# A soft mixture of experts: the first layer of experts 1 to 7 from seven block products instead of eight

## The chip, the cores and the metric

The kernel runs on one core of a Trainium2 chip. The metric is device microseconds of one execution, launch to end. The kernel before takes 835.61 us, the median of 3 runs (835.45 to 835.63).

## The reference, cut to what matters

Eight sequences of 512 tokens and width 256 go through an attention layer and then a soft mixture of 8 experts. Its first half makes dispatch and combine weights and gives each expert 128 slots per sequence, 1024 slots in all. Then, for every expert e:

```
h  = einsum('besd,edh->besh', slots, w1) + b1      # 1024 slots, 256 -> 1024
h  = gelu(h)
eo = einsum('besh,ehd->besd', h, w2) + b2          # 1024 -> 256
out = einsum('bmd,bnm->bnd', eo, combine)
```

The last layer norm takes each row's mean away, so the kernel centres w2 and b2 over the output width beforehand (subtracts each row's mean). Arithmetic is float32. TensorE is given each operand as two float32r parts, a rounded high part and the low part that the rounding left, and three passes are summed: high x high, high x low, low x high (`PASSES`).

## The kernel before, in words

The engines' programs are written out one after the other by hand; there is no scheduler. Each engine runs its instructions in the written order and waits on semaphores. The stages are attention (to about 160 us), dispatch and combine weights (to 380 us), the experts (380 to 737 us) and the combine stage (to the end). The change touches the experts.

An expert has two halves f of 512 slots (four sequences each). `KH` is 8, the number of 128-wide blocks of the hidden width, `KD` is 2, the number of 128-deep blocks of the input width. For each of its 16 tiles i = (f, j) TensorE makes a hidden tile of 128 hidden units x 512 slots (`hidden`, L1014): 2 input blocks x 3 passes = 6 matmuls of 512 columns. ScalarE applies gelu from PSUM into `act` (L1495) and rounds it into the high part of `act_r` (L1500). VectorE subtracts to get the low part (`rest_of_act`, L2121). Two tiles later TensorE multiplies it with w2 (`expert_out`): for each of 4 sequences one matmul of 512 columns, the activation's high part against both parts of w2 side by side (L1044), and one of 256 columns, its low part against w2's high part (L1047). Only the first half of expert 0 uses three matmuls of 256 columns instead (`narrow_out`, L1022). After the last block VectorE adds the two column halves and the bias into `slots_eo` (`keep_eo`, L2144 and L2150, 8 instructions a half).

Beside that, for the expert after, VectorE sums w2's rows (L2173) and subtracts their mean (L2184), ScalarE rounds both weights (L1465) and VectorE makes their low parts (L2078); VectorE also rounds and splits the slots (L2085, L2089). Rounded weights have two sets of tiles, one for each parity of the expert; the loops hold two experts. GpSimd does nothing in this stage: its last work is in the stage before, where it scales dispatch weights (L617), makes low parts of y (L624) and centres rows (L630). SP (the DMA queue's engine) loads the raw weights of an expert when those of the one before are split.

## Time and profile before

| what | us |
|---|---|
| median of 3 runs | 835.61 |
| the profiled execution, its own time | 835.44 |
| its span, first to last instruction | 833.3 |
| TensorE busy | 826.1 (99%) |
| VectorE busy | 643.3 (77%) |
| ScalarE busy | 548.2 (66%) |
| GpSimd busy | 86.7 (10%) |

Shares of busy time are averages over the four stages. The granted TensorE clock is 1.00 of full speed (2.4 GHz) in every stretch. A matmul's shown duration is longer than its pace, since the next starts before it ends; the pace is read from the chain of waits.

### The profile page before, as it was taken

Reading aid. Unit: us, or ns where it says so; the run is one execution under the profiler, and the core shown is the slowest. Engines: PE = TensorE matmul, PEld = TensorE weight load, DVE = VectorE, ACT = ScalarE, POOL = GpSimd, SP = SyncE. Lnnn points to the kernel's source line nnn. Section 1 sums busy time; section 2 is a strip of 40 time slices with the busy share of each in tenths; the row PEclk is TensorE's granted clock in tenths of the full one; section 3 lists DMA queues with packets and bytes.
Section 4 is the critical chain, followed back from the end, with each engine's and each line's share of the span. In section 5 each row is a group of like instructions: output and inputs, shape, how many; then the busy total and the mean of one; then the engine's idle time right before and its main releaser. Section 6 shows DMA issues by size and latency. Waiting matters only on the chain.

```text
span 833.3 us, 14932 instructions
## 1 busy us (share of the span) xinstructions
PE 826.1 (99%) x4866; PEld 717.7 (86%) x4866; DVE 643.3 (77%) x1293; ACT 548.2 (66%) x1078; POOL 86.7 (10%) x103
## 2 busy tenths in 40 slices
PE   8999999999999999999999999999999999999997
PEld 8989999888888888878888888888888888899997
DVE  8788888899999999998867666665766665477776
ACT  5676766657787887689555565555555554568775
POOL 0300000033223334350000000000000000000000
PEclk9999999999999999999999999999999999999999
DMA  6111131102223252225030202020110203066893
GB/s 209 59 51 52 53 99 33 45 28 101 102 94 121 98 192 102 76 77 203 1 102 0 101 1 101 0 98 3 45 55 2 99 1 101 1 217 210 282 292 111
DMA packets 52562, 75.38 MB, mean 90 GB/s; under 512 B 3104, under 2 KB 33696, under 8 KB 52384
## 3 DMA queue, kind: packets, MB, share of 16 engines
q1 hardware_dynamic: 52512, 74.76, 26.8%
q8 instruction: 26, 0.43, 0.2%
q14 instruction: 24, 0.20, 0.1%
HBM read 49.59 MB, written 25.17 MB: 90 GB/s over the span
## 4 chain that ended last, share of the span: by engine, by line
PE 96%; DVE 2%; ACT 1%; issue 1%; DMA 0%; ACTq 0%; DVEq 0%
PE bank L1014 21%; PE bank L1044 13%; PE bank L1086 11%; PE bank L883 10%; PE bank L908 10%; PE bank L1047 7%; PE bank L892 3%; PE bank L750 3%; PE bank L800 3%; PE bank L693 2%; PE bank L773 2%; PE bank L761 2%; PE bank L783 2%; PE bank L715 1%; PE bank L726 1%; PE bank L1022 1%
## 5 line engine op out<-in xcount | busy, mean ns | idle before, releaser
L1014 PE MATMUL bank<-snT,w_r 128*128 128x512 f32 x768 | 194.7, 393 | 0.0
L1495 ACT ACTIVATE act<-bank,b_sb 128x512 f32<-128x512 f32 x128 | 88.0, 687 | 139.3 <-PE bank L1014 138.9
L2121 DVE TENSOR_TENSOR act_r<-act,act_r 128x512 fp32r<-128x512 f32 x128 | 88.3, 691 | 110.7 <-ACT act_r L1500 110.6
L1044 PE MATMUL bank<-w_r,act_r 128*128 128x512 f32 x480 | 173.1, 396 | 0.0
L1014 PEld LDWEIGHTS bank<-snT,w_r 128*128 128x128 f32 x768 | 136.5, 188 | 28.8 <-issue 0.3
L1047 PE MATMUL bank<-w_r,act_r 128*128 128x256 f32 x480 | 134.6, 280 | 0.0
L1044 PEld LDWEIGHTS bank<-w_r,act_r 128*128 128x128 f32 x480 | 90.2, 188 | 21.0
L908 PE MATMUL bank<-disp_r,y_r 128*128 128x512 f32 x384 | 103.4, 406 | 0.4 <-DVE disp_r L1974 0.3
L883 PE MATMUL bank<-yT_r,snT 128*128 128x512 f32 x384 | 99.4, 395 | 0.0
L1047 PEld LDWEIGHTS bank<-w_r,act_r 128*128 128x128 f32 x480 | 90.6, 189 | 4.1
L1086 PE MATMUL bank<-eo_r,comb_r 128*128 128x258 f32 x768 | 92.3, 282 | 0.0
L1086 PEld LDWEIGHTS bank<-eo_r,comb_r 128*128 128x128 f32 x768 | 92.2, 189 | 0.1
L1500 ACT ACTIVATE act_r<-act 128x512 fp32r<-128x512 f32 x128 | 80.9, 632 | 12.0
L883 PEld LDWEIGHTS bank<-yT_r,snT 128*128 128x128 f32 x384 | 71.7, 188 | 15.9 <-issue 0.5
L908 PEld LDWEIGHTS bank<-disp_r,y_r 128*128 128x128 f32 x384 | 67.7, 189 | 12.8 <-DVE disp_r L1974 0.8
L1367 ACT ACTIVATE disp<-neg_lt,neg_max 128x512 f32<-128x512 f32 x56 | 40.5, 723 | 35.6 <-DVE neg_lt L1940 35.4
L617 POOL TENSOR_SCALAR disp<-disp,rz_disp 128x512 f32<-128x512 f32 x56 | 39.6, 707 | 123.9 <-DVE rz_disp L1969 123.9
L1974 DVE TENSOR_TENSOR disp_r<-bank,disp_r 128x512 fp32r<-128x512 f32 x64 | 43.6, 682 | 5.0 <-ACT disp_r L1379 4.4
L1394 ACT ACTIVATE comb<-comb,zero_col 128x512 f32<-128x512 f32 x64 | 45.3, 715 | 1.6 <-DVE comb L1963 1.4
L1379 ACT ACTIVATE disp_r<-bank 128x512 fp32r<-128x512 f32 x64 | 37.4, 585 | 10.7 <-PE bank L892 10.7
L1940 DVE TENSOR_SCALAR_CACHE_REDUCE neg_lt<-bank 128x512 f32<-128x512 f32 x56 | 38.3, 684 | 4.7 <-DVE comb L1963 2.5
L2078 DVE TENSOR_TENSOR w_r<-stage,w_r 128x1024 fp32r<-128x1024 f32 x32 | 38.9, 1218 | 0.0
(203 smaller groups left out, 1311.3 us busy)
## 6 DMA issues: line engine op xcount, KB each, us to landing
combine_scratch<-comb SPq DMA_DIRECT2D x64, 256.0 KB, 2.0
stage<-in_w SPq DMA_DIRECT2D x16, 1024.0 KB, 6.3
stage<-combine_scratch SPq DMA_DIRECT2D x4, 2048.0 KB, 9.0
snT<-combine_scratch SPq DMA_DIRECT2D x4, 2048.0 KB, 9.6
x_scratch<-stage SPq DMA_DIRECT2D x8, 512.0 KB, 3.2
x<-x_scratch SPq DMA_DIRECT2D x8, 512.0 KB, 3.9
x_d<-x_scratch SPq DMA_DIRECT2D x8, 512.0 KB, 9.5
slots_eo<-in_x SPq DMA_DIRECT2D x7, 512.0 KB, 4.4
```

The source lines that it names most:

```text
L883: last = pe.matmul(bank[m % 2][:, :], snT[:, i, k, m * S:(m + 1) * S], yT_r[:, j, k, :], start=(n == 0), stop=(n == len(steps) - 1))
L908: last = pe.matmul(bank[4 + k][:, :], y_r[:, i, t, k * P:(k + 1) * P], disp_r[h][:, j, t, :], start=(n == 0), stop=(n == len(fill_steps) - 1))
L1014: last = pe.matmul(hidden_bank(e, i)[:, :], w1_r[q][:, a, k, j * P:(j + 1) * P], sl_r[f][:, c, k, :], start=(n == 0), stop=(n == len(steps ...
L1044: pe.matmul(bank[BH + c][:, :].rearrange("p (w d) -> p w d", w=2), act_r[:, i % RING, 0, c * S:(c + 1) * S], w2_r[q][:, :, j, :], start=(j ...
L1047: pe.matmul(bank[BH + c][:, 0:D], act_r[:, i % RING, 1, c * S:(c + 1) * S], w2_r[q][:, 0, j, :], start=False, stop=(j == KH - 1), skip_gro ...
L1086: done = pe.matmul(bank[4 * u + t][:, 0:DZ], comb_r[:, m % RING, i, t * P:(t + 1) * P], eo_r[u][:, j, m, :], start=(m == 0 and n == 0), st ...
L1367: act_fn(dispatch(b, m), neg_logits(b, m), ACT.Exp, bias=least, scale=-1.0, accum_out=total).then_inc(disp_exp, 1)
L1394: act_fn(comb[:, m % RING, :], comb[:, m % RING, :], ACT.Exp, bias=zero_col[:], scale=-1.0)\
L1495: act_fn(act[:, i % 2, :], hidden_bank(e, i)[:, :], ACT.Gelu, bias=b1_sb[:, ds(e * KH + i % KH, 1)])\
L1500: act_fn(act_r[:, i % RING, 0, :], act[:, i % 2, :], ACT.Copy).then_inc(h_hi, 1)
L1974: v.tensor_tensor(disp_r[h][:, 1, :, cols], bank[2 + m % 2][:, :].rearrange("p (t s) -> p t s", t=NT), disp_r[h][:, 0, :, cols].bitcast(F3 ...
L2121: v.tensor_tensor(act_r[:, i % RING, 1, :], act[:, i % 2, :], act_r[:, i % RING, 0, :].bitcast(F32), ALU.subtract).then_inc(h_split, 1)
```

## The change

Expert 0 stays as it was, but for its second half, whose second layer now also uses three matmuls of 256 columns. In experts 1 to 7 the first layer is cut into a 2 x 2 x 2 block problem: two input blocks k, two halves f of the slots, and hidden blocks in pairs (g, g + 4), so that a `group` g of 4 has four hidden tiles. Winograd's form of Strassen's scheme makes these four tiles from seven products instead of eight. A product (`product`) is 3 matmuls of 512 columns over one 128-deep block.

- The operands of the products are sums: three sums of slots and S1 to S4 of w1's blocks. GpSimd makes them: 4 subtractions of 128x512 for an expert (`combine_slots`) and 4 of 128x128 for each group (`combine_w1`).
- ScalarE rounds them (w1: 128x512 and 128x384 a group; slots: two pairs and two singles an expert), VectorE makes the low parts. The slots' last operand is rounded by VectorE (`split_last_operand`).
- Four products run into one chain bank (bank 0 or 2 by the group's parity). On the way ScalarE copies the partial sum three times (`keep_part`): into bank 3, into the tile `act[3]` or `act[4]`, into `act[2]`. VectorE adds bank 1 to the two copies in SBUF (`add_tile`). Gelu then reads bank 3, `act[2]`, the chain bank and `act[3]` or `act[4]`.
- w2 is centred while it is rounded: ScalarE's Identity takes minus the mean as bias, VectorE's low part adds it in one scalar_tensor_tensor. The instruction L2184 goes.
- `expert_out` is three matmuls of 256 columns for each sequence and tile, 12 a tile, and the four banks 4 to 7 hold both halves, so `keep_eo` is 2 instructions of 128x512 a half. The rounded w2 has one set of tiles instead of two. The loops hold one expert, in groups of four.

On TensorE a group reads: P0, P3, out tile 0 of the group before, P1, P2, out tile 1, P4, out tile 2, P5, P6, out tile 3. P1 and P2 wait for the first copy, P4 for the second, P5 for the third, P6 for `add_tile` 0, and P3 of the next group for `add_tile` 1 (both use bank 1).

```diff
+        ORDER = [0, 3, 1, 2, 4, 5, 6]
+        TILE_OF = [0, 2, 1, 3]
+        OUT_NEEDS = [1, 3, 3, 4]
+        ALL_PRODUCTS = HALVES * KH + (E - 1) * GROUPS * PRODUCTS
...
+            def combine_slots(e):
+                if not is_batch(e, 1):
+                    pool.wait_ge(sl_split, right_through(e - 1, 5))
+                t1, t2, t3, t4 = sl_sum[:, 3], sl_sum[:, 0], sl_sum[:, 1], sl_sum[:, 2]
+                at = 4 * (e - 1)
...
+                nc.gpsimd.tensor_tensor(t3, slots_raw(e, 1, 1), slots_raw(e, 0, 1), ALU.subtract)\
+                    .then_inc(sl_summed, 1)
+                pool.wait_ge(sl_summed, at + 1)
+                alone(pool)
+                nc.gpsimd.tensor_tensor(t1, slots_raw(e, 0, 1), slots_raw(e, 0, 0), ALU.subtract)\
+                    .then_inc(sl_summed, 1)
+                pool.wait_ge(sl_summed, at + 2)
+                alone(pool)
+                nc.gpsimd.tensor_tensor(t2, slots_raw(e, 1, 1), t1, ALU.subtract).then_inc(sl_summed, 1)
+                pool.wait_ge(sl_summed, at + 3)
+                alone(pool)
+                nc.gpsimd.tensor_tensor(t4, slots_raw(e, 1, 0), t2, ALU.subtract).then_inc(sl_summed, 1)
...
+            def combine_w1(e, g):
+                pool.wait_ge(w_loaded[0], 16 * (e + 1))
+                if not is_batch(e, 1) or g >= 2:
+                    pool.wait_ge(w_split[0], fills_through(e, g - 2, 2))
+                s2, s3, s4 = [w1_sum[:, g % 2, n, :] for n in range(3)]
...
+            def expert(e, last=False):
+                combine_w1(e, 1)
+                combine_w1(e, 2)
+                if not last:
+                    combine_slots(e + 1)
+                combine_w1(e, 3)
+                if not last:
+                    combine_w1(e + 1, 0)
...
+            def product(e, g, n):
+                if n in (0, 2):
+                    pe.wait_ge(w_split[0], fills_through(e, g, 1 + n // 2))
+                if g == 0:
+                    pe.wait_ge(sl_split, right_through(e, 1 if is_batch(e, 1) and n == 0 else [2, 2, 3, 2, 4, 4, 5][n]))
+                if n == 3 and is_batch(e, 1) and g == 0:
+                    pe.wait_ge(h_act, HALVES * KH - 1)
+                elif n == 3:
+                    pe.wait_ge(tile_added, added_through(e, g, 0))
+                elif n in (1, 2, 4, 5):
+                    pe.wait_ge(part_kept, parts_through(e, g, {1: 1, 2: 1, 4: 2, 5: 3}[n]))
+                elif n == 6:
+                    pe.wait_ge(tile_added, added_through(e, g, 1))
+                x = chain_bank(g)
+                target = [x, bank[3], x, bank[1], x, x, bank[1]][n]
+                for s, (a, c) in enumerate(PASSES):
+                    done = pe.matmul(target[:, :], w1_op[:, g % 2, a, LEFT_AT[n], :], slot_operand(n)[:, c, :],
+                                     start=(n in (0, 3) and s == 0), stop=(s == 2), skip_group_check=True)
+                done.then_inc(h_in_psum, 1)
...
+            def expert_out(e, g, a):
+                pe.wait_ge(h_split, tiles_through(e, g, OUT_NEEDS[a]))
+                if a == 0:
+                    pe.wait_ge(w_split[1], w2_through(e, g + 1))
+                if g == 0 and a % 2 == 0:
+                    pe.wait_ge(eo_ready, e * HALVES * BH - (BH if a == 0 else 0))
+                j = g + GROUPS if a in (1, 2) else g
+                out_rows(a // 2, a, j, g == 0 and a % 2 == 0, g == GROUPS - 1 and a % 2 == 1)
+            def expert_group(e, g, before):
+                product(e, g, 0)
+                product(e, g, 3)
+                before(0)
+                product(e, g, 1)
+                product(e, g, 2)
+                before(1)
+                product(e, g, 4)
+                before(2)
+                product(e, g, 5)
+                product(e, g, 6)
+                before(3)
...
+            def keep_part(e, g, i):
+                sc.wait_ge(h_in_psum, products_through(e, g, [1, 4, 5][i]))
+                if i == 1:
+                    sc.wait_ge(h_split, tiles_through(e, g, -1))
+                to = [bank[3][:, :], kept_tile(g, 3), act[:, 2, :]][i]
+                act_fn(to, chain_bank(g)[:, :], ACT.Copy).then_inc(part_kept, 1)
+            def gelu(e, g, i):
+                tile = TILE_OF[i]
+                source = [bank[3][:, :], act[:, 2, :], chain_bank(g)[:, :], kept_tile(g, 3)][i]
+                if i in (0, 2):
+                    sc.wait_ge(h_in_psum, products_through(e, g, 3 if i == 0 else 6))
+                    sc.wait_ge(h_split, tiles_through(e, g, 0 if i else -1 if is_batch(e, 1) and g == 0 else -3))
+                else:
+                    sc.wait_ge(tile_added, added_through(e, g, 1 + i // 2))
+                j = g + GROUPS if i in (1, 2) else g
                 alone(sc)
-                act_fn(act[:, i % 2, :], hidden_bank(e, i)[:, :], ACT.Gelu, bias=b1_sb[:, ds(e * KH + i % KH, 1)])\
-                    .then_inc(h_act, 1)
-                sc.wait_ge(h_act, n + 1)
-                if i >= RING or not first:
-                    sc.wait_ge(eo_steps, (n - RING + 1) * BH)
-                act_fn(act_r[:, i % RING, 0, :], act[:, i % 2, :], ACT.Copy).then_inc(h_hi, 1)
+                act_fn(kept_tile(g, tile), source, ACT.Gelu, bias=b1_sb[:, ds(e * KH + j, 1)]).then_inc(h_act, 1)
...
+            def rest_of_w1(e, g, step):
+                dve.wait_ge(w_hi[0], fills_through(e, g, step + 1))
+                cols = slice(4 * step, 4 + 3 * step)
+                v.tensor_tensor(w1_op[:, g % 2, 1, cols, :], w1_sum[:, g % 2] if step else w1_direct(g),
+                                w1_op[:, g % 2, 0, cols, :].bitcast(F32), ALU.subtract).then_inc(w_split[0], 1)
...
+            def expert_group(e, g, first=False, last=False):
+                keep_part(e, g, 0)
+                if g == 0:
+                    cast_pair(e, 1)
+                if g:
+                    gelu(e, g - 1, 3)
+                    round_tile(e, g - 1, 3)
+                elif not first:
+                    gelu(e - 1, GROUPS - 1, 3)
+                    round_tile(e - 1, GROUPS - 1, 3)
+                if 0 < g < GROUPS - 1:
+                    round_w1(e, g + 1, 0)
+                    round_w1(e, g + 1, 1)
+                elif g and not last:
+                    cast_slots(e + 1, 3)
+                    cast_pair(e + 1, 0)
+                keep_part(e, g, 1)
+                gelu(e, g, 0)
+                round_tile(e, g, 0)
+                keep_part(e, g, 2)
+                if g == 0:
+                    round_w1(e, 1, 0)
+                    round_w1(e, 1, 1)
+                if g < 2:
+                    round_w2(e, g)
+                elif g == GROUPS - 1 and not last:
+                    round_w1(e + 1, 0, 0)
+                    round_w1(e + 1, 0, 1)
+                gelu(e, g, 1)
+                round_tile(e, g, 1)
+                if g == 1:
+                    round_w2(e, 2)
+                gelu(e, g, 2)
+                round_tile(e, g, 2)
+                if g == 1:
+                    round_w2(e, 3)
+                if g == GROUPS - 1 and not last:
+                    cast_slots(e + 1, 2)
...
+            def add_tile(e, g, i):
+                tile = 2 + i
+                dve.wait_ge(part_kept, parts_through(e, g, 3))
+                if i:
+                    dve.wait_ge(h_in_psum, products_through(e, g, 7))
+                v.tensor_tensor(kept_tile(g, tile), bank[1][:, :], kept_tile(g, tile), ALU.add).then_inc(tile_added, 1)
...
+                if g:
+                    rest_of_tile(e, g - 1, 3)
+                elif not first:
+                    rest_of_tile(e - 1, GROUPS - 1, 3)
+                if g == 0:
+                    split_last_operand(e)
+                elif g < GROUPS - 1:
+                    rest_of_w1(e, g + 1, 0)
+                    rest_of_w1(e, g + 1, 1)
+                elif not last:
+                    rest_of_operand(e + 1, 3)
+                    rest_of_pair(e + 1, 0)
+                rest_of_tile(e, g, 0)
+                add_tile(e, g, 0)
+                if g == 0:
+                    if not first:
+                        keep_eo(e - 1, 0)
+                    rest_of_w1(e, 1, 0)
+                    rest_of_w1(e, 1, 1)
+                elif g == 1:
+                    rest_of_w2(e, 1)
+                elif g == GROUPS - 1 and not last:
+                    rest_of_w1(e + 1, 0, 0)
+                add_tile(e, g, 1)
+                if g == 0:
+                    rest_of_w2(e, 0)
+                rest_of_tile(e, g, 1)
+                if g == 1:
+                    rest_of_w2(e, 2)
+                    rest_of_w2(e, 3)
+                elif g == 2 and not last:
+                    sum_rows(e + 1, 0)
+                elif g == GROUPS - 1 and not last:
+                    rest_of_w1(e + 1, 0, 1)
+                    rest_of_operand(e + 1, 2)
```

The first place where instructions move is TensorE's program at the head of an expert in the loop, before (`w1_r1`: rounded w1 of the odd expert; bank 4 to 7: outputs):

```order
L1014 MATMUL bank0<-snT,w1_r1 128x512 [waits h_act]
L1014 MATMUL bank0<-snT,w1_r1 128x512 x5
L1030 ISA
L1044 MATMUL bank4<-w2_r0,act_r 128x512 [waits h_split]
L1047 MATMUL bank4<-w2_r0,act_r 128x256
L1044 MATMUL bank5<-w2_r0,act_r 128x512
L1047 MATMUL bank5<-w2_r0,act_r 128x256
```

and now, from P5 of group 0 to the first output tile in group 1 (`w1_op`: operands from w1; `w1_first`: slot operands 4 to 6):

```order
L1201 MATMUL bank0<-w1_first,w1_op 128x512 [waits part_kept]
L1201 MATMUL bank0<-w1_first,w1_op 128x512 x2
...
L1201 MATMUL bank1<-w1_first,w1_op 128x512 [waits tile_added]
L1201 MATMUL bank1<-w1_first,w1_op 128x512 x2
...
L1201 MATMUL bank2<-snT,w1_op 128x512 [waits w1_split]
...
L1201 MATMUL bank1<-snT,w1_op 128x512 [waits tile_added]
...
L1211 ISA [waits w2_split]
L1159 MATMUL bank4<-w2_r,act_r 128x256 [waits eo_ready]
```

Where a hidden tile waited only for gelu and an output tile only for its activation, the products now wait for copies (`part_kept`), additions (`tile_added`) and, at a group's head, for the split weights.

The second place is VectorE's program around the end of group 0, before (one tile's low part after another, with the weights of the next expert between them):

```order
L2121 TENSOR_TENSOR act_r<-act,act_r 128x512 [waits h_hi]
L2182 REGISTER_ALU
L2184 TENSOR_TENSOR stage<-stage,w_mean 128x1024 [waits w2_summed]
L2120 REGISTER_ALU
L2121 TENSOR_TENSOR act_r<-act,act_r 128x512 [waits h_hi]
L2077 REGISTER_ALU
L2078 TENSOR_TENSOR w_r<-stage,w_r 128x1024 [waits w1_hi]
```

and now, from the low part of tile 0 of group 0 to that of tile 2 (L2454), with both `add_tile` (L2448), `keep_eo` (L2466), the low parts of w1's next group (L2406) and of w2 (L2413):

```order
L2454 TENSOR_TENSOR act_r<-act,act_r 128x512 [waits h_hi]
...
L2448 TENSOR_TENSOR act<-bank,act 128x512 [waits part_kept]
...
L2466 TENSOR_TENSOR slots_eo<-bank,b_bc 128x512
...
L2466 TENSOR_TENSOR slots_eo<-bank,b_bc 128x512
...
L2406 TENSOR_TENSOR w_op<-stage,w_op 128x512 [waits w1_hi]
L2404 REGISTER_ALU
L2406 TENSOR_TENSOR w_op<-w_sum,w_op 128x384 [waits w1_hi]
L2447 ISA [waits part_kept]
L2448 TENSOR_TENSOR act<-bank,act 128x512 [waits h_in_psum]
L2411 REGISTER_ALU
L2413 SCALAR_TENSOR_TENSOR w_r<-stage,w_mean,w_r 128x256 [waits w2_hi]
```

The second `add_tile` stands behind two instructions on w1 and the first rows of w2 behind it. The third place is GpSimd, whose program had nothing here and now holds, for the slots of the next expert, behind the last split of this expert's slots (`sl_split`):

```order
L736 ISA [waits sl_split]
L736 ISA
L736 TENSOR_TENSOR sl_sum<-slots_eo 128x512
...
L740 TENSOR_TENSOR sl_sum<-slots_eo 128x512
L742 REGISTER_ALU
L744 TENSOR_TENSOR sl_sum<-slots_eo,sl_sum 128x512 [waits sl_summed]
...
L747 TENSOR_TENSOR sl_sum<-slots_eo,sl_sum 128x512
```

Each waits for the one before it. Behind them stand the w1 sums of group 3.

## Rows read from the trace of the kernel before

**Rows 1.** The page, part 1: busy us, share of the span, instructions.

```profile
PE 826.1 (99%) x4866; PEld 717.7 (86%) x4866; DVE 643.3 (77%) x1293; ACT 548.2 (66%) x1078; POOL 86.7 (10%) x103
```

**Rows 2.** Stages: busy us of PE, PEld, DVE, ACT, POOL; clock; DMA share; GB/s.

```profile
450.00:500.00 50.00, 50.00 (x253) 42.19 (x253) 33.69 (x55) 28.48 (x42) 0.00 (x0) 1.00 0.13 43
```

**Rows 3.** Chain that ended last, in order of time: start, us, what.

```profile
392.76 2.87 PE bank L1022 x24
...
405.53 2.75 PE bank L1014 x12
...
433.37 1.40 PE bank L1014 x6
...
455.65 1.40 PE bank L1014 x6
```

**Rows 4.** Groups by line and form, 420 to 730 us: busy, mean ns, idle before.

```profile
L2121 DVE TENSOR_TENSOR act_r<-act,act_r 128x512 fp32r<-128x512 f32 x112 | 77.4, 691 | 101.6 <-ACT act_r L1500 101.5
L1495 ACT ACTIVATE act<-bank,b_sb 128x512 f32<-128x512 f32 x111 | 76.3, 688 | 128.0 <-PE bank L1014 128.0
L1500 ACT ACTIVATE act_r<-act 128x512 fp32r<-128x512 f32 x111 | 70.1, 632 | 11.4
L2078 DVE TENSOR_TENSOR w_r<-stage,w_r 128x1024 fp32r<-128x1024 f32 x25 | 30.5, 1218 | 0.0
L1465 ACT ACTIVATE w_r<-stage 128x1024 fp32r<-128x1024 f32 x24 | 25.1, 1046 | 0.0
```

**Rows 5.** Groups by line and form, whole span: other prices.

```profile
L1379 ACT ACTIVATE disp_r<-bank 128x512 fp32r<-128x512 f32 x64 | 37.4, 585 | 10.7 <-PE bank L892 10.7
...
L1963 DVE TENSOR_TENSOR comb<-neg_lt,bank 128x512 f32<-128x512 f32 x56 | 37.4, 674 | 0.2
...
L1818 DVE SCALAR_TENSOR_TENSOR stage<-stage,rstd,slots_eo 128x256 f32<-128x256 f32 x32 | 13.9, 489 | 1.4 <-DVE rstd L1814 0.9
...
L1403 ACT ACTIVATE w_row<-stage 128x256 f32<-128x256 f32 x8 | 3.3, 408 | 0.0
...
L2129 DVE TENSOR_TENSOR slots_eo<-bank,b_bc 128x512 f32<-128x512 f32 x2 | 1.3, 684 | 0.0
```

**Rows 6.** Timeline at 502 us, loop of experts: start, us, engine, instruction.

```profile
502.54 0.63 ACT L1500 ACTIVATE act_r<-act 128x512 fp32r<-128x512 f32 x1
...
503.08 1.05 ACT L1465 ACTIVATE w_r<-stage 128x1024 fp32r<-128x1024 f32 x1
503.20 0.69 DVE L2121 TENSOR_TENSOR act_r<-act,act_r 128x512 fp32r<-128x512 f32 x1 [0.74 <-ACT act_r L1500]
503.81 1.22 DVE L2078 TENSOR_TENSOR w_r<-stage,w_r 128x1024 fp32r<-128x1024 f32 x1
...
504.22 0.39 PE L1044 MATMUL bank<-w_r,act_r 128*128 128x512 f32 x1
...
504.51 0.69 ACT L1495 ACTIVATE act<-bank,b_sb 128x512 f32<-128x512 f32 x1 [0.39 <-PE bank L1014]
...
505.32 0.63 ACT L1500 ACTIVATE act_r<-act 128x512 fp32r<-128x512 f32 x1
```

**Rows 7.** Timeline of GpSimd, 192 to 253 us.

```profile
194.55 1.30 POOL L624 TENSOR_TENSOR y_r<-y,y_r 128x512 fp32r<-128x512 f32 x1
...
250.66 1.72 POOL L624 TENSOR_TENSOR y_r<-y,y_r 128x512 fp32r<-128x512 f32 x1
252.69 0.69 POOL L617 TENSOR_SCALAR disp<-disp,rz_disp 128x512 f32<-128x512 f32 x1 [0.30 <-DVE rz_disp L1969]
```

**Rows 8.** Timeline of VectorE, 194 to 254 us.

```profile
194.82 1.58 DVE L1954 TENSOR_TENSOR run_min<-run_min,neg_lt 128x512 f32<-128x512 f32 x1
...
250.34 0.89 DVE L1954 TENSOR_TENSOR run_min<-run_min,neg_lt 128x512 f32<-128x512 f32 x1
251.16 0.68 DVE L1974 TENSOR_TENSOR disp_r<-bank,disp_r 128x512 fp32r<-128x512 f32 x1
...
253.58 0.68 DVE L1954 TENSOR_TENSOR run_min<-run_min,neg_lt 128x512 f32<-128x512 f32 x1
```

More of the change, by code:

```diff
@@ L1050, in expert @@
-            def expert(e, q, first=False):
-                for i in range(HALVES * KH):
-                    if i % KH != 3:
-                        hidden(e, q, i, first)
-                    if i % KH == 2 and not (first and i == 2):
-                        hidden(e, q, i + 1, first)
-                    if first and i == 3:
-                        hidden(e, q, i, first)
-                    for n in FIRST_OUTS.get(i, [i - 2]) if first else [i - 2]:
-                        if n >= 0:
-                            expert_out(e, q, n, first)
-                        else:
-                            expert_out(e - 1, 1 - q, HALVES * KH + n)
@@ L1065, in _ @@
-            expert(0, 0, first=True)
-            with pe.Fori(0, E // 2 - 1) as it:
-                expert(2 * it + 1, 1)
-                expert(2 * it + 2, 0)
-            expert(E - 1, 1)
-            for i in range(2):
-                expert_out(E - 1, 1, HALVES * KH - 2 + i)
+                out_rows(f, i % RING, j, j == 0, j == KH - 1)
+            for i in range(HALVES * KH):
+                if i % KH != 3:
+                    hidden(i)
+                if i % KH == 2 and i != 2:
+                    hidden(i + 1)
+                if i == 3:
+                    hidden(i)
+                for n in FIRST_OUTS.get(i, [i - 2]):
+                    first_out(n)
@@ new lines, in expert @@
+            def expert(e, first=False):
+                if first:
+                    product(e, 0, 0)
+                    first_out(HALVES * KH - 2)
+                    product(e, 0, 3)
+                    product(e, 0, 1)
+                    product(e, 0, 2)
+                    first_out(HALVES * KH - 1)
+                    product(e, 0, 4)
+                    product(e, 0, 5)
+                    product(e, 0, 6)
+                else:
+                    expert_group(e, 0, lambda a: expert_out(e - 1, GROUPS - 1, a))
+                for g in range(1, GROUPS):
+                    expert_group(e, g, lambda a: expert_out(e, g - 1, a))
@@ L1074, in combine @@
+            expert(1, first=True)
+            with pe.Fori(2, E) as e:
+                expert(e)
+            for a in range(TILES):
+                expert_out(E - 1, GROUPS - 1, a)
             def combine(b, u, last=False):
@@ L1538, in _ @@
-            expert(0, 0, first=True)
-            with sc.Fori(0, E // 2 - 1) as it:
-                expert(2 * it + 1, 1)
-                expert(2 * it + 2, 0)
-            expert(E - 1, 1, last=True)
-            experts_finished(sc)
+            for i in range(HALVES * KH):
+                activate(i)
+                if i == 0:
+                    keep_slots(B - 1, 1, 1)
+                if i == KH:
+                    weights_finished(sc)
+                    round_w1(1, 0, 0)
+                    round_w1(1, 0, 1)
+                if i == KH + 3:
+                    cast_pair(1, 0)
@@ new lines, in _ @@
+            for g in range(GROUPS):
+                expert_group(1, g, first=(g == 0))
+            with sc.Fori(2, E - 1) as e:
+                for g in range(GROUPS):
+                    expert_group(e, g)
+            for g in range(GROUPS):
+                expert_group(E - 1, g, last=True)
+            gelu(E - 1, GROUPS - 1, 3)
+            round_tile(E - 1, GROUPS - 1, 3)
+            sc.wait_ge(h_in_psum, ALL_PRODUCTS)
+            sc.wait_ge(w_split[1], w2_through(E, 0))
+            round_eo(0, 0, 0)
@@ L1545, in square_mix @@
+            for m in range(BEGUN_COMBINE):
+                round_combine(0, 0, m, True)
+            sc.wait_ge(eo_ready, E * HALVES * BH - BH)
+            round_eo(0, 0, 1)
             def square_mix(b, u, t):
@@ L1557, in combine @@
             def combine(b, u, first=False, last=False):
-                for m in range(BEGUN if first else 0, E):
+                for m in range(BEGUN_COMBINE if first else 0, E):
                     round_combine(b, u, m, first)
@@ new lines, in _ @@
+            for g in range(GROUPS):
+                expert_group(1, g, first=(g == 0))
+            with dve.Fori(2, E - 1) as e:
+                for g in range(GROUPS):
+                    expert_group(e, g)
+            for g in range(GROUPS):
+                expert_group(E - 1, g, last=True)
+            rest_of_tile(E - 1, GROUPS - 1, 2)
+            rest_of_tile(E - 1, GROUPS - 1, 3)
+            dve.wait_ge(h_in_psum, ALL_PRODUCTS)
+            pad_eo(0)
+            rest_of_eo(dve, 0, 0, 0)
@@ L2270, in combine @@
             def combine(b, u, first=False, last=False):
-                for m in range(BEGUN if first else 0, E):
+                for m in range(BEGUN_COMBINE if first else 0, E):
                     rest_of_combine(b, u, m)
```

476 lines of the change are left out of this document (277 added, 199 removed).

## The prediction

> **What bounds the kernel now.** I read the page's busy times first: TensorE 99%, VectorE 77%, ScalarE 66% of the span [rows 1]. Then the table by stages: inside the experts TensorE is busy 50.00 of 50 us, VectorE 33.69, ScalarE 28.48, GpSimd 0 [rows 2]. The reader sees that TensorE sets the stage's length alone and nothing ever makes it wait. So the question is what its own stream costs, and whether the work that the change puts on the other three engines stays out of its way.
>
> TensorE's prices come from the chain, where each piece is the pace and not the modelled duration. Twelve 512-column matmuls take 2.75 us, six 1.40 [rows 3]; I take 0.231 us each, 0.6925 for a product of three. 24 narrow matmuls of 256 columns take 2.87, so 12 take 1.435 [rows 3]. Half an expert is 455.65 - 433.37 = 22.28 us [rows 3], so an expert 44.56; with 16 hidden tiles of 1.385 that leaves 1.40 for one tile of the second layer in its present form.
>
> **The change on TensorE.** In an expert: 28 products x 0.6925 = 19.39, and 16 output tiles x 1.435 = 22.96, together 42.35. Before 44.56. The hidden layer gives 16 x 1.385 - 19.39 = 2.77, the narrower second layer takes 0.56 back. Gain 2.21 an expert, 15.5 for seven. Expert 0's second half gets the narrow form in 8 tiles: + 0.3. Sum -15.2. From the profiled execution's 835.44 (0.17 under the median of 835.61) that makes 820.2, if TensorE never waits.
>
> **What now stands beside it.** A group has a period of 42.35/4 = 10.59 us. Counting from the head of a group: P0 ends 0.69, P3 1.38, out tile 0 2.82, P1 3.51, P2 4.20, out 1 5.64, P4 6.33, out 2 7.76, P5 8.45, P6 9.14, out 3 10.58. From one matmul after a hidden tile to gelu's start is 504.51 - 504.22 = 0.29 [rows 6]; I use it for every release by TensorE.
>
> ScalarE in an expert: 16 gelus of 0.688 and 16 roundings of 0.632 [rows 4], 12 partial copies, 4 x (512 + 384 columns) of w1, 8 x 256 of w2, two pairs of 1024 and two single operands of slots. A copy reads PSUM as L1379 does in 0.585 [rows 5]. Its form from bank to bank is in no row: the bounds are 0.54, the pace at which ScalarE takes an instruction that waits for nothing (503.08 - 502.54, [rows 6]), and 0.688; I take 0.585. 384 columns are 0.5, between 0.408 [rows 5] and 0.632; a w2 block with a bias 0.408; a pair 1.046 [rows 4]. Sum 11.0 + 10.1 + 7.0 + 4.5 + 3.3 + 2.1 + 1.3 = 39.3 of 42.35, less about 0.09 wherever an instruction follows without a wait. Full, but it fits. What it must do in time: the second copy can start at 4.20 + 0.29 and ends at 5.1, P4 is due at 5.64; the third starts at 6.62, ends at 7.2, P5 is due at 7.76. Margins are near 0.5 us and 0.2 in group 3, where a pair of slots has to wait for P1 (3.80) and ends only at 4.8. Gelu to its rounding is 0.81 in the loop [rows 6]; with that the program still arrives in time at every copy. I cost it at nothing, with up to 0.3 us a group (28 groups, 8.4) as the other end.
>
> VectorE in an expert: 16 low parts of 0.691 [rows 4], 8 additions and 4 `keep_eo` of 0.68 (L1963, L2129, [rows 5]), w1's low parts 4 x (0.69 + 0.55), w2's 8 x 0.49 (L1818), slots' about 5.0, sums of w2 2.6: 35.6, or 32 at the pace of 0.61 (503.81 - 503.20, [rows 6]). Alone it fits too.
>
> **GpSimd is the term that counts.** It now makes 4 sums of 128x512 an expert and 4 of 128x128 a group. A tensor_tensor of 128x512 costs it 1.30 [rows 7]. A 128-column one is in no row; the bounds are a quarter of that, 0.33, and 1.30; I take 0.5. The rows show what it does to VectorE. At 194.55 GpSimd starts a tensor_tensor; VectorE's L1954, two operands in SBUF, starts at 194.82 and takes 1.58, while alone it takes 0.68 [rows 7, 8]: it finishes 0.55 after GpSimd's end, so it stood for the whole of it. At 250.34 VectorE is first: GpSimd's sum, started at 250.66, takes 1.72 instead of 1.30, as it first waits for VectorE's end. The next instruction, L1974, reads PSUM and SBUF and takes 0.68 in the middle of GpSimd's work [rows 8]. So two-operand SBUF work of the two engines goes one after the other, an instruction at a time; VectorE's `add_tile` and `keep_eo` are free of that, its low parts are not.
>
> The Trainium skill, SBUF — State Buffer, section "Who interferes with whom", says the same of the shared port pair: whoever starts first has it for the whole instruction, the other blocks fully. By that rule the trace agrees, with 1.58 against 0.68. It speaks against putting sums on GpSimd beside a VectorE that is 80% busy; it does not say who goes next when both wait.
>
> Place: end of group 0, where the slots' sums of the next expert are released by this expert's last slot split. ScalarE ends the pair at about 2.5, tile 3's rounding at 3.9; VectorE's low part of it ends 4.6, the last operand's copy and low part 5.7. GpSimd starts at 6.0 (0.30 as in [rows 7]); between its dependent sums I put 0.2.
> - Sum 1: 6.0 to 7.3. VectorE's low part of tile 0, ready at 6.5, runs 7.3 to 7.9. Sum 2: 7.9 to 9.2. `add_tile` 0: 7.9 to 8.5; P6 due 8.45, late 0.15.
> - `keep_eo` to 9.8. Sum 3: 9.4 to 10.7. w1's first low part: 10.7 to 11.3; P0 of group 1, due 10.58, is 0.8 late.
> - Sum 4 and w1's second low part now both wait. If VectorE goes on: low part to 11.75, `add_tile` 1 to 12.35, so P3 (due 11.27) is 1.2 late; sum 4 11.75 to 13.0; w2's low parts to 13.85; the first output tile of group 1, due 11.96, starts at 13.95. Late 2.0 in all, and behind it nothing else comes late: groups 1 to 3 have 7 to 9 us of VectorE work in 10.6.
>
> Without the sums the same program ends w1's low parts at 10.3, `add_tile` 1 at 10.9 and w2's at 1.1 of group 1, just in time. So the wait is GpSimd's. In the bodies of experts 2 to 6 it costs 2.0; in expert 1 the `keep_eo` in between is missing (1.25), so 0.8; expert 7 has no slots' sums. 5 x 2.0 + 0.8 = 10.8. The ends are 0 (the sums fall into gaps) and 5 x 3.0 + 1.8 = 17, below.
>
> The rest costs nothing, and this is the cover: the raw weights load in group 2 and are needed in group 3, a group of 10.6 us away; expert 0's second half gives ScalarE and VectorE less work than an expert does; the combine stage finds its first rounded rows while TensorE still has 4 output tiles (5.7 us) to do.
>
> Sum: 820.2 + 10.8 = 831.0.
>
> **Rivals.**
> 1. The shared access hardly matters: GpSimd's sums fall where VectorE waits or reads PSUM. For it: VectorE has 7 to 10 us an expert idle and the late chain hangs on the phase of four instructions; a shift of 0.3 us frees it. Against: [rows 8]. Time 820.2 + 1 to 4, so about 822.
> 2. GpSimd goes first when both wait, and the w1 sums of group 3 then cut in as well. Sum 4 runs 11.3 to 12.5, w1's second low part ends at 13.0, `add_tile` 1 at 13.6, w2's at 14.4 plus up to 0.5: late 3.0. 5 x 3.0 + 1.8 = 17: 837. For it: it waited longer. With the small lateness of rival 3 (0.1 a group, 3 us) it is 840, slower than before. It decides once the wait an expert is over 2.2 us: 15.2/7.
> 3. ScalarE becomes the bound: 39.3 of 42.35 in strict order, with 12 copies that TensorE waits for. With 0.3 us late in each of 28 groups it adds 8.4 to the sum: 839. For it: margins of 0.2 to 0.5; against: its pace of 0.54 gives back 3 to 5 us an expert.
>
> **How the numbers follow.** My forecast (826 to 834.5) 0.33; rival 1 (820 to 826) 0.27; rival 2 0.20; rival 3 0.15; 0.05 for a loss that I have not seen. The predicted time is 831.0; its own range 826 to 835. Over all: low 821, high 842, which leaves some 0.1 on each side. 0.2% is 1.7 us, about what a measurement can tell from none. Faster, below 833.9: rival 1 and nearly all of the forecast's, 0.57. Within: 0.12, from the upper end of the forecast and the lower of rivals 2 and 3. Slower: 0.31.
>
> **What would show it.** In the profile after, three-matmul products pace at 0.69 us and output tiles at 1.43; an expert's period is 42.3 plus its waits, so 44.4 in the loop. TensorE's waits stand at the product line and the narrow output line, released by VectorE (w1's low part, `add_tile`, w2's low part), once an expert and at the head of group 1. GpSimd's 128x512 sums show over 1.3 us, and VectorE's low parts beside them well over 0.69. Expert 7 has none of it. Wrong would be: waits spread over all groups and released by ScalarE's copies (rival 3), a period of 42.4 (rival 1), of 45.4 or more with GpSimd first (rival 2), or products slower than 0.69, since then the gain itself is misjudged.

## The result, and the profile after

The changed kernel takes 837.26 us (median of 9 runs, 837.13 to 838.84), the kernel before 835.54 in the same comparison: ratio 1.0025, 95% interval 1.0015 to 1.0035. It is slower by 1.7 us. Two of its nine executions took 838.8 us, at a mean clock of 0.997 and 0.998 where the other seven had 0.999 to 1.000. Forecast were 831.0 and "faster". The time lies inside the stated range of 821 to 842, on the wrong side of the line.

The page's first part, and the stage table for 50 us in the loop of experts; they answer to [rows 1] and [rows 2]:

```profile
PE 817.7 (98%) x5262; PEld 726.9 (87%) x5262; DVE 698.6 (84%) x1343; ACT 632.6 (76%) x1274; POOL 202.5 (24%) x243
```

```profile
500.00:550.00 50.00, 48.26 (x308) 42.96 (x307) 42.27 (x59) 40.39 (x71) 20.91 (x27) 1.00 0.12 42
```

TensorE is now idle in the experts, 1.74 us of 50. The granted clock is 1.00 in this stretch, so nothing is lost there. What TensorE waited for, 420 to 730 us (us in total, times, longest):

```profile
PE bank L1201 <- DVE act L2448: 8.5, 11, 1.2
PE bank L1201 <- ACT act L1684: 0.8, 1, 0.8
PE bank L1159 <- issue: 0.5, 1, 0.5
PE bank L1201 <- DVE w_op L2406: 0.5, 3, 0.2
```

L1201 is a product, L1159 an output tile, L2448 `add_tile`, L2406 a low part of w1, L1684 a copy of a partial sum. VectorE is the releaser fourteen times of sixteen, eleven times with `add_tile`. "issue" is a wait to which the profile can put no releaser. These idle times leave out what the modelled end of the matmul before covers, so the loss is better read from the timeline of one expert in the loop. TensorE, from P0 and P3 of group 0 to the first output tile in group 1 (a piece can hold two products; x is the number of instructions in it, the bracket is the idle time just before it and what ended it):

```profile
510.35 1.55 PE L1201 MATMUL bank<-snT,w_op 128*128 128x512 f32 x6
...
518.12 0.86 PE L1201 MATMUL bank<-w_first,w_op 128*128 128x512 f32 x3
519.25 0.96 PE L1201 MATMUL bank<-w_first,w_op 128*128 128x512 f32 x3 [0.27 <-DVE act L2448]
520.05 1.59 PE L1159 MATMUL bank<-w_r,act_r 128*128 128x256 f32 x12
521.79 0.96 PE L1201 MATMUL bank<-snT,w_op 128*128 128x512 f32 x3
523.94 0.97 PE L1201 MATMUL bank<-snT,w_op 128*128 128x512 f32 x3 [1.19 <-DVE act L2448]
525.03 1.70 PE L1159 MATMUL bank<-w_r,act_r 128*128 128x256 f32 x12
```

GpSimd over the same time: the four slots' sums and the first w1 sum behind them:

```profile
516.75 1.29 POOL L736 TENSOR_TENSOR sl_sum<-slots_eo 128x512 f32 x1 [2.02 <-DVE w_first L2399]
518.28 1.46 POOL L740 TENSOR_TENSOR sl_sum<-slots_eo 128x512 f32 x1 [0.24 <-POOL sl_sum L736]
519.89 1.29 POOL L744 TENSOR_TENSOR sl_sum<-slots_eo,sl_sum 128x512 f32<-128x512 f32 x1
521.41 1.46 POOL L747 TENSOR_TENSOR sl_sum<-slots_eo,sl_sum 128x512 f32<-128x512 f32 x1 [0.23 <-POOL sl_sum L744]
523.44 0.45 POOL L757 TENSOR_TENSOR w_sum<-stage 128x128 f32<-128x128 f32 x1 [0.56 <-DVE w_op L2406]
```

VectorE over the same time (L2454 low parts of tiles, L2466 `keep_eo`, L2413 low parts of w2):

```profile
516.80 1.80 DVE L2454 TENSOR_TENSOR act_r<-act,act_r 128x512 fp32r<-128x512 f32 x1 [0.39 <-ACT act_r L1704]
518.52 0.68 DVE L2448 TENSOR_TENSOR act<-bank,act 128x512 f32<-128x512 f32 x1
519.12 1.27 DVE L2466 TENSOR_TENSOR slots_eo<-bank,b_bc 128x512 f32 x2
520.32 1.42 DVE L2406 TENSOR_TENSOR w_op<-stage,w_op 128x512 fp32r<-128x512 f32 x1
521.65 1.63 DVE L2406 TENSOR_TENSOR w_op<-w_sum,w_op 128x384 fp32r<-128x384 f32 x1
523.21 0.68 DVE L2448 TENSOR_TENSOR act<-bank,act 128x512 f32<-128x512 f32 x1
523.81 1.07 DVE L2413 SCALAR_TENSOR_TENSOR w_r<-stage,w_mean,w_r 128x256 fp32r<-128x256 f32 x2
```

Three low parts of VectorE take 1.80, 1.42 and 1.63 us where they take 0.69 or 0.55 alone. Each ends 0.4 to 0.6 us after a sum of GpSimd, the first after 518.04, the second after 521.18, the third after 522.87. The additions and `keep_eo`, which read PSUM, keep 0.68 and 1.27 for two. Counting from the group's head at 510.35, P6 is due at 518.80 and starts 0.45 late, P3 of group 1 is due at 521.62 and starts 2.3 late, the output tile is due at 522.31 and starts 2.7 late. The same P3 of the expert before stands at 478.80; the period is 523.94 - 478.80 = 45.14 us, against 42.35 for TensorE's own work and 44.56 before.

The decisive moment is at 521.4 to 521.7. Sum 4 was ready at 521.41, while VectorE still worked on w1's first low part (to 521.74); it waited 0.17 us (1.46 instead of 1.29). VectorE's second low part was the next in its own row and would have begun at 521.65. GpSimd went first, and VectorE got the access at 522.87. The bodies of experts 2, 4, 5 and 6 show the same order: each time sum 4 takes 1.46 or 1.47 us and w1's second low part 1.64.

### The profile page after: what moved, and what is told of

It reads as the page before. It is cut to its first block, busy times and chain, and to the rows that moved or that the text cites. A ratio compares the mean times of both kernels' runs of the same rounds, so it can differ in the third digit from the quotient of the medians.

```text
span 835.4 us, 16740 instructions
## 1 busy us (share of the span) xinstructions
PE 817.7 (98%) x5262; PEld 726.9 (87%) x5262; DVE 698.6 (84%) x1343; ACT 632.6 (76%) x1274; POOL 202.5 (24%) x243
## 4 chain that ended last, share of the span: by engine, by line
PE 87%; DVE 6%; issue 4%; ACT 2%; DVEq 1%; DMA 0%; ACTq 0%
PE bank L1159 19%; PE bank L1201 13%; PE bank L1264 11%; PE bank L1022 10%; PE bank L1047 10%; PE bank L1031 3%; PE bank L889 3%; PE bank L939 3%; PE bank L1151 3%; PE bank L832 2%; PE bank L912 2%; PE bank L900 2%; PE bank L922 2%; PE bank L854 1%; PE bank L865 1%
## 5 line engine op out<-in xcount | busy, mean ns | idle before, releaser
L1159 PEld LDWEIGHTS bank<-w_r,act_r 128*128 128x128 f32 x1536 | 199.5, 191 | 13.4 <-issue 3.8
L1159 PE MATMUL bank<-w_r,act_r 128*128 128x256 f32 x1536 | 203.6, 283 | 1.1 <-issue 0.5
L2454 DVE TENSOR_TENSOR act_r<-act,act_r 128x512 fp32r<-128x512 f32 x112 | 89.3, 804 | 25.0 <-ACT act_r L1704 24.9
L1201 PE MATMUL bank<-snT,w_op 128*128 128x512 f32 x336 | 89.1, 398 | 7.9 <-DVE act L2448 7.2
L1201 PEld LDWEIGHTS bank<-snT,w_op 128*128 128x128 f32 x336 | 59.1, 189 | 21.1 <-DVE act L2448 9.8
L1201 PE MATMUL bank<-w_first,w_op 128*128 128x512 f32 x252 | 68.9, 397 | 2.1 <-DVE act L2448 1.4
L2448 DVE TENSOR_TENSOR act<-bank,act 128x512 f32<-128x512 f32 x56 | 38.5, 688 | 21.8 <-PE bank L1201 20.0
L757 POOL TENSOR_TENSOR w_sum<-stage 128x128 f32<-128x128 f32 x28 | 14.8, 528 | 161.0 <-DMA stage<-in_w 115.5
L1201 PEld LDWEIGHTS bank<-w_first,w_op 128*128 128x128 f32 x252 | 43.4, 190 | 10.4 <-DVE act L2448 3.5
L1684 ACT ACTIVATE act<-bank 128x512 f32<-128x512 f32 x56 | 33.2, 593 | 22.7 <-PE bank L1201 21.5
L1697 ACT ACTIVATE act<-act,b_sb 128x512 f32<-128x512 f32 x56 | 40.2, 718 | 12.1 <-DVE act L2448 11.0
```

The lines of the kernel that those rows point to most:

```text
L1159: done = pe.matmul(bank[BH + 2 * f + c // 2][:, (c % 2) * D:(c % 2 + 1) * D], act_r[:, tile, a, c * S:(c + 1) * S], w2_r[:, w, j, :], star ...
L1201: done = pe.matmul(target[:, :], w1_op[:, g % 2, a, LEFT_AT[n], :], slot_operand(n)[:, c, :], start=(n in (0, 3) and s == 0), stop=(s == 2 ...
L1697: act_fn(kept_tile(g, tile), source, ACT.Gelu, bias=b1_sb[:, ds(e * KH + j, 1)]).then_inc(h_act, 1)
L2454: v.tensor_tensor(act_r[:, tile, 1, :], kept_tile(g, tile), act_r[:, tile, 0, :].bitcast(F32), ALU.subtract).then_inc(h_split, 1)
```

## The experiments

Ten kernels were run, each beside the kernel before. Its median was 835.47 to 835.54 in every comparison, so the times can be set beside one another and beside 837.26.

**GpSimd's slots' sums left out.** Theory A was by then: these sums cause the whole wait at the head of group 1.

```diff
                 combine_w1(e, 2)
-                if not last:
-                    combine_slots(e + 1)
                 combine_w1(e, 3)
...
-                sc.wait_ge(sl_summed, 4 * (e - 1) + 4)
+                sc.wait_ge(sl_summed, 4)
```

> The changed kernel without GpSimd's four 128x512 sums of slots for experts 2 to 7 (left out; the operands then hold expert 1's sums). Theory A: these sums, which shut VectorE's low parts out one instruction at a time, are the whole wait of 2.8 us an expert at the head of group 1. In experts 2 to 6 it goes, in expert 1 most of it too: about 837.3 - 16 = 821, period of a loop expert 42.4 instead of 45.1. Theory B: VectorE is too full at the end of group 0 by itself (9.3 us of work in 10.6, in chains): the wait stays for the larger part, 832 or more. Theory C: ScalarE's copies come late: nothing changes, 837.

Measured: 821.83 us, ratio 0.9835 (0.9819 to 0.9851). TensorE's waits that are left, 420 to 740 us:

```profile
PE bank L1199 <- ACT act L1682: 0.8, 1, 0.8
PE bank L1157 <- issue: 0.3, 1, 0.3
PE bank L1199 <- DVE act L2446: 0.2, 1, 0.2
```

All three are single waits. Theory A holds: 15.4 us of the 837.26 are these sums. VectorE's load (B) and ScalarE's copies (C) are not the limit. A loop expert has the period 42.35 here (516.92 - 474.57, the same products one expert apart). It also checks the sum for TensorE alone: 821.83 less 1.3 is 820.5, forecast 820.2.

**All four sums in a row, from the first product of group 2.**

```diff
                     pool.wait_ge(sl_split, right_through(e - 1, 5))
+                    pool.wait_ge(h_in_psum, products_through(e - 1, 2, 1))
...
                 combine_w1(e, 2)
+                combine_w1(e, 3)
                 if not last:
                     combine_slots(e + 1)
-                combine_w1(e, 3)
```

> The changed kernel complete, with the slots' sums moved on GpSimd behind the w1 sums of group 3 and released by the first product of group 2 instead of by the last slot split in group 0. Theory A: group 2 is the one in which VectorE has least to do (some 7 us of 10.6), so the sums' shutting out is absorbed there: TensorE's waits fall from 2.8 us an expert to under 0.3, 820.5 to 822.5. Theory B: no better than 832, since VectorE's own work at the end of group 0 stays. A third possibility: the same wait turns up at the head of group 3, 830 or more.

Measured: 833.12 us, ratio 0.9972 (0.9961 to 0.9982). That is 10.6 us above the range of theory A, whose expectation was wrong. TensorE's wait had moved:

```profile
PE bank L1160 <- DVE act_r L2455: 9.8, 6, 1.7
```

and VectorE shows why (L2414 the last low parts of w2, L2455 those of tiles 1 and 3), with sum 3 on GpSimd and the output tile on TensorE:

```profile
488.56 2.43 DVE L2414 SCALAR_TENSOR_TENSOR w_r<-stage,w_mean,w_r 128x256 fp32r<-128x256 f32 x2 [1.03 <-ACT w_r L1724]
490.92 3.45 DVE L2455 TENSOR_TENSOR act_r<-act,act_r 128x512 fp32r<-128x512 f32 x2
...
490.86 1.26 POOL L745 TENSOR_TENSOR sl_sum<-slots_eo,sl_sum 128x512 f32<-128x512 f32 x1
...
492.73 1.70 PE L1160 MATMUL bank<-w_r,act_r 128*128 128x256 f32 x12 [1.68 <-DVE act_r L2455]
```

The head of group 2 holds two-operand SBUF work only: w2's last low parts and two tiles' low parts. Two low parts took 3.45 us instead of 1.3. The second output tile of the group needs the first of them (`OUT_NEEDS`), which could only run behind sum 3, and that ended at 492.12; the tile starts at 492.73, where 489.50 + 1.39 = 490.89 was its time. "The group with the least work" was the wrong measure.

**The second w1 low part behind the second addition.**

```diff
                     rest_of_w1(e, 1, 0)
-                    rest_of_w1(e, 1, 1)
...
                 add_tile(e, g, 1)
                 if g == 0:
+                    rest_of_w1(e, 1, 1)
                     rest_of_w2(e, 0)
```

> The changed kernel with VectorE's second w1 low part of group 0 moved behind the second addition. Theory A: P3 of group 1, 2.3 us late before, is 0.8 late, but w2's low part, for which the output tile waits, still stands behind both and behind sum 4: the tile starts 0.2 to 0.4 us earlier, 6 times: 835 to 836. If only the addition's lateness mattered (theory D: the last wait is P3's), 1.5 us an expert would go: 828.

Measured: 834.26 us, ratio 0.9988 (0.9979 to 0.9998), 3.0 under the changed kernel, more than expected of A and far less than of D. The waits:

```profile
PE bank L1159 <- DVE w_r L2413: 5.0, 5, 1.0
PE bank L1159 <- issue: 1.7, 1, 1.7
PE bank L1201 <- DVE act L2448: 1.4, 5, 0.3
```

P3's wait is gone (the 1.4 is that of P6, five times 0.27), that for w2's low part stands in its place: putting VectorE's own work in another order hands the lateness on. The wait of 1.7 under "issue" is by its time the same one in expert 1: w2's low parts end at 434.53, the output tile starts at 434.63. The execution traced took 835.66 us, 1.4 over the median: after the waits of 0.78 and 1.70 in expert 1 the granted clock was 0.50, the lower level, from 436 to 438 us.

**One part of the change alone: the narrow second layer in the kernel before.**

```diff
-                if first and f == 0:
-                    narrow_out(q, i, j)
-                    return
+                if j == 0 and not first:
+                    pe.wait_ge(eo_ready, (e * HALVES + f - 1) * BH)
+                narrow_out(q, i, j, f)
+                return
```

(`narrow_out` writes banks 4 and 5 or 6 and 7 by the half; `keep_eo` is that of the changed kernel.)

> The kernel before with one part of the change alone: the second layer as three matmuls of 256 columns for each sequence and tile in all experts, and its outputs in four half-filled banks kept by two additions. By the prices of the chain, 1.435 against 1.40 us a tile, 16 tiles in 7 experts and 8 in expert 0: 120 x 0.035 = 4.2 us more, 839.7. If the narrow form paid only for its columns (both forms have 768), 835.5.

Measured: 838.99 us, ratio 1.0041 (1.0027 to 1.0055), 3.5 us more; 4.2 were worked out. Its chain shows the tile at 1.43:

```profile
433.74 1.39 PE bank L1014 x6
435.12 1.43 PE bank L1022 x12
436.56 1.39 PE bank L1014 x6
437.94 1.43 PE bank L1022 x12
```

Three matmuls of 256 columns cost more than one of 512 and one of 256, though the columns are the same.

**The sums parted and put where VectorE reads PSUM.** Now theory A1 was: not the amount of shutting out counts, but which instruction of VectorE it meets.

```diff
-            def combine_slots(e):
+            def combine_slots(e, part=(0, 1, 2, 3), g=None):
+                if g is not None:
+                    pool.wait_ge(h_split, tiles_through(e - 1, g, 1))
...
                 if not last:
-                    combine_slots(e + 1)
+                    combine_slots(e + 1, (0,), 0)
                 combine_w1(e, 3)
+                if not last:
+                    combine_slots(e + 1, (1,), 1)
+                if not last:
+                    combine_slots(e + 1, (2, 3), 2)
```

> The changed kernel complete, the four slots' sums on GpSimd parted: the first released by the low part of tile 0 in group 0, the second by that of group 1, two by that of group 2, so that they start when VectorE goes on with additions from PSUM, which they do not shut out. Theory A1 (the place in VectorE's program decides): TensorE's waits go but for a few tenths an expert: 822 to 824. Theory A2 (the amount decides: 5.8 us of sums an expert are taken from VectorE wherever they are): 830 or more, as with all four in group 2.

Measured: 821.82 us, ratio 0.9838 (0.9822 to 0.9854). It computes everything and equals the kernel without the sums. Of TensorE's waits, 420 to 740 us, one is left:

```profile
PE bank L1201 <- ACT act L1684: 0.8, 1, 0.8
```

GpSimd's two sums in group 2, and VectorE over the same time:

```profile
492.46 1.29 POOL L743 TENSOR_TENSOR sl_sum<-slots_eo,sl_sum 128x512 f32<-128x512 f32 x1 [9.32 <-DVE act_r L2454]
493.98 1.29 POOL L743 TENSOR_TENSOR sl_sum<-slots_eo,sl_sum 128x512 f32<-128x512 f32 x1 [0.23 <-POOL sl_sum L743]
```

```profile
491.54 0.69 DVE L2454 TENSOR_TENSOR act_r<-act,act_r 128x512 fp32r<-128x512 f32 x1 [0.98 <-ACT act_r L1704]
492.21 0.69 DVE L2448 TENSOR_TENSOR act<-bank,act 128x512 f32<-128x512 f32 x1
494.40 0.69 DVE L2448 TENSOR_TENSOR act<-bank,act 128x512 f32<-128x512 f32 x1 [1.50 <-PE bank L1201]
495.01 0.81 DVE L2454 TENSOR_TENSOR act_r<-act,act_r 128x512 fp32r<-128x512 f32 x1
```

Between the two low parts VectorE does two additions from PSUM and waits 1.50 us for TensorE anyway; the sums lie in that and cost the next low part 0.12 us. The sum of group 1 (at 481.83) does meet w2's low parts, 1.40 us for two instead of 0.88; TensorE does not wait for it.

**The same with the reordered w1 low part.** Edit: both edits above together.

> As e7_gaps, and in addition the second w1 low part of group 0 behind the second addition. Theory A1: the first sum can still delay w1's low parts by some tenths in group 0; with the addition in front P3 is never late: equal to e7_gaps or up to 1 us better, 821.5 to 823.5. Theory A2: 828 to 831.

Measured: 822.10 us, ratio 0.9840 (0.9823 to 0.9856): no gain left for it, as P3 is not late any more.

**VectorE makes the slots' sums itself, in group 2.**

```diff
                 add_tile(e, g, 0)
+                if g == 2 and not last:
+                    combine_slots(e + 1, (0, 1))
...
                 elif g == 2 and not last:
+                    combine_slots(e + 1, (2, 3))
                     sum_rows(e + 1, 0)
```

(GpSimd's call of `combine_slots` is taken out; VectorE has the function with the same four subtractions.)

> The changed kernel complete, with the slots' sums of experts 2 to 7 on VectorE itself, two behind each of the low parts of tiles 0 and 2's neighbours in group 2: 4 x 0.69 us more work for VectorE, none of the shutting out by GpSimd's long sums. Theory A: VectorE's total stays under TensorE's, its work in group 2 grows from some 7 to 9.5 us, and group 3 starts up to 1.5 us late on it: 822 to 826. If VectorE's load were the limit (theory B), 832 or more.

Measured: 825.12 us, ratio 0.9876 (0.9860 to 0.9893). TensorE waits five times for an addition, 1.5 us in all as far as idle time shows it. VectorE can carry the work, but not as cheaply as GpSimd in the gaps.

**The sums cut to 128 columns** for experts 2 to 7, in number and place as in the changed kernel.

```diff
+                n = slice(0, 512 if is_batch(e, 1) else 128)
...
-                nc.gpsimd.tensor_tensor(t3, slots_raw(e, 1, 1), slots_raw(e, 0, 1), ALU.subtract)\
+                nc.gpsimd.tensor_tensor(t3[:, n], slots_raw(e, 1, 1)[:, n], slots_raw(e, 0, 1)[:, n], ALU.subtract)\
```

> The changed kernel with GpSimd's slots' sums of experts 2 to 7 cut to 128 columns instead of 512 (the other columns are left out), in their place and number. One takes 0.46 us instead of 1.29. If the length of one sum sets the wait, low parts lose at most 0.5 us each and the last sum ends before w1's low parts begin: 823 to 825. If the number of handovers sets it: 832 or more.

Measured: 822.55 us, ratio 0.9847 (0.9831 to 0.9864). As many sums, a third of the length: the wait is gone. The number of sums is not what costs. In the loop the first two still meet the low part of tile 0 (0.97 us); the last ends before w1's low parts, which take 0.68 and 0.55, so this run does not part the length of a sum from what it then meets.

**All four sums in a row, started by the low part of tile 0 of group 2.** The edit is that of the parted sums with one call, `combine_slots(e + 1, (0, 1, 2, 3), 2)`, behind `combine_w1(e, 3)`.

> The changed kernel complete, all four slots' sums in a row on GpSimd, started by the low part of tile 0 of group 2, so 3 to 4 us later in the same group than in e1_late. The amount and the length of a sum are those of e1_late (833.1). By the theory that the place in VectorE's program decides: the first two run beside the additions, the third and fourth meet the low parts of tiles 2 and 1, of which TensorE needs the last only at 4.2 us of group 3: 822 to 824. If a row of four is what costs: 830 or more.

Measured: 822.48 us, ratio 0.9843 (0.9827 to 0.9860). Against 833.12 this is the same row of sums in the same group, only later in it. The second sum stretches one low part (1.03 us instead of 0.69), and TensorE does not wait for it. The place in VectorE's program decides, by 10.6 us.

**Sums added to the kernel before.**

```diff
+            with pool.Fori(1, E) as e:
+                pool.wait_ge(h_in_psum, e * HALVES * KH + 4)
+                for n in range(4):
+                    alone(pool)
+                    nc.gpsimd.tensor_tensor(spare[:], flat, flat, ALU.subtract).then_inc(spared, 1)
+                    pool.wait_ge(spared, 4 * (e - 1) + n + 1)
```

> The kernel before with GpSimd work added and nothing else: in each of experts 1 to 7 four dependent sums of 128x512 from SBUF (of b2's rows, into a spare tile that nobody reads), started by the 4th hidden tile. They shut VectorE's low parts out as in the changed kernel. By the theory of place: a low part there ends 2.5 us after its hidden tile, and TensorE wants it 4.2 us after, so a block of 1.3 us is absorbed: 835.5, no difference, with low parts of up to 2 us in the trace. If the sharing cost by its amount: 7 x 5.2 us of blocks, 840 or more.

Measured: 835.42 us, ratio 0.9999 (0.9990 to 1.0009). Low parts of tiles and GpSimd's sums, 420 to 730 us; the first line answers to L2121 of [rows 4]:

```profile
L2132 DVE TENSOR_TENSOR act_r<-act,act_r 128x512 fp32r<-128x512 f32 x112 | 86.3, 773 | 92.8 <-ACT act_r L1511 92.6
```

```profile
L655 POOL TENSOR_TENSOR spare<-b_bc 128x512 f32<-128x512 f32 x28 | 33.1, 1182 | 298.5 <-PE bank L1025 295.5
```

The low parts took 86.3 - 77.4 = 8.9 us longer, and the kernel not at all: there TensorE has two tiles of other work before it needs one. In each of the four experts read, two low parts meet the sums (2.87 us for two instead of 1.3); the later sums of the four run beside a row sum of w2 with one operand in SBUF, which keeps 1.20 to 1.21 us. So 8.9 us of blocks were tested, not the 36 that the expectation reckoned with.

## Why the prediction was wrong

**TensorE's own stream: right.** Products and output tiles pace as priced (1.39 for two products, 1.43 a tile, in the chain of the changed kernel). The bare sum was 820.2; the run without the sums gives 821.8 with 1.3 us of single waits in it, as far as idle time shows them. The narrow form's price was 3.5 us measured alone, 4.2 in the forecast (seven times 0.56, and 0.3 in expert 0).

**ScalarE at nothing: right in the loop.** Copies took 0.580 into a bank and 0.593 into SBUF, priced 0.585:

```profile
L1684 ACT ACTIVATE act<-bank 128x512 f32<-128x512 f32 x56 | 33.2, 593 | 22.7 <-PE bank L1201 21.5
...
L1684 ACT ACTIVATE bank<-bank 128x512 f32<-128x512 f32 x28 | 16.2, 580 | 8.6 <-PE bank L1201 8.5
```

In all of the stage TensorE waited for a copy once, 0.8 us in expert 1. Rival 3 is out.

**The wait of GpSimd's making: right in mechanism and place, wrong in size.** The walk put the slots' sums at 6.0, 7.9, 9.4 and the fourth beside w1's second low part; the trace has them at 6.4, 7.9, 9.5 and 11.1 from the group's head. The step that failed is "if VectorE goes on". Where both engines waited, I let VectorE's next instruction go ahead of sum 4; the trace shows GpSimd first. That was the stated fork to rival 2, with 3.0 us an expert, and 2.8 were measured (45.14 - 42.35). Five loop experts make 14.0 instead of 10.0. The w1 sums of group 3 also met w2's low parts, as rival 2 said, but for little: 1.07 us for two instead of 0.88.

**Expert 1: the other part of the miss.** I gave it 0.8, for want of `keep_eo`. Its P3 of group 1 starts here:

```profile
429.57 1.66 PE L1201 MATMUL bank<-w_first,w_op 128*128 128x512 f32 x6 [0.78 <-ACT act L1684]
431.13 0.96 PE L1201 MATMUL bank<-snT,w_op 128*128 128x512 f32 x3
433.29 0.97 PE L1201 MATMUL bank<-snT,w_op 128*128 128x512 f32 x3 [1.20 <-DVE act L2448]
434.75 1.67 PE L1159 MATMUL bank<-w_r,act_r 128*128 128x256 f32 x12 [0.49 <-issue]
```

In expert 1 no output tile stands between P4 and P5, so the third copy is waited for in full. From its first product at 422.31 to the first output tile of group 1 at 434.75 TensorE has 9.1 us of work (nine products, two tiles) and took 12.4: 3.3 late. The run without the sums took 11.1 for the same stretch (422.44 to 433.54), 2.0 late: 0.8 idle for the copy, and then `add_tile` and w2's low parts, which end at 433.43. So 2.0 of the 3.3 are a wait that the prediction put at nothing ("just in time"), and 1.3 are the sums', where it had 0.8. Here sum 3 was the one that stood waiting (ready at 430.67) and went ahead of w1's second low part.

The sum with these sizes is 820.2 + 14.0 + 3.3 = 837.5; measured 837.26. The sums' own part is 14.0 + 1.3 = 15.3, and leaving them out gave 15.4.

**What the forecast should have taken.** With both ends of the fork written down, 2.0 and 3.0 an expert on either side of the break-even of 2.2, the choice between them was a guess. No row of the kernel before shows the fork: where its L624 waited for VectorE, VectorE's next instruction read PSUM (L1974, [rows 7, 8]). The only reason on either side stood with rival 2, that GpSimd had been waiting longer. The fork alone would not have made it slower: 820.2 + 14.0 + 0.8 = 835.0, still 0.5 us under the kernel before. The 2.5 us more in expert 1 do that. The expectation for the sums moved to group 2 repeated the fault in another form: it counted VectorE's load by the group, not which instruction would be met.

## What to carry to other kernels

That GpSimd is idle does not make the work put on it free: with operands in SBUF it holds up VectorE's two-operand SBUF instructions for the length of its own. Find in VectorE's program the stretch in which it reads PSUM or waits, and release GpSimd's instruction by the one just ahead of it; the same sums cost 15 us at the end of group 0 and nothing there. The faster product scheme paid 1.6% (821.82 against 835.50) once that was done. Where two prices on either side of the break-even hang on who goes first, give both the chance that an unknown deserves.

## What the runs showed of the hardware

- A tensor_tensor of 128x512 from SBUF on GpSimd takes 1.29 us in the changed kernel, one of 128x128 0.45 (both in the timeline above); 0.5 had been taken for the second.
- While it runs, VectorE's subtraction of two SBUF operands stands still; an addition with one operand in PSUM keeps 0.68 us. The Trainium skill, SBUF — State Buffer, section "Who interferes with whom", has the rule, that whoever issues first has the shared ports for the whole instruction; it leaves open which engine goes first when both wait. Here GpSimd's sum, ready while VectorE was still busy, went ahead of the instruction that stood next in VectorE's row, once in each of experts 1 to 6, six times of six (521.41 to 522.87 us in the timeline above).
- A row sum on VectorE (TENSOR_REDUCE, one operand in SBUF) keeps 1.21 us beside GpSimd's sums (at 496.55 us in the run with all four in a row).
- ScalarE copies 128x512 from PSUM to PSUM in 0.580 us, from PSUM to SBUF in 0.593.
- TensorE's granted clock fell once right after waits: to 0.50 from 436 to 438 us, in the trace of the run "The second w1 low part behind the second addition", after 0.78 and 1.70 us of idle time. In the changed kernel's trace, with 0.78, 1.20 and 0.49 in the same place, it stayed at 1.00. What decides it no run shows.
